# Order of expert weight loads and of the first chunk's statistics, and one filling of the expert slots, in a graph network kernel

## The reference

```python
edge_index = jnp.stack([src, dst])
x = x + L0_gnn(layernorm(x), edge_index, ...)    # two graph convolutions
x = x + L0_ffn(layernorm(x), ...)                # 8 experts, 2 of them for each row
x = x + L1_gnn(layernorm(x), edge_index, ...)    # two graph convolutions
x = x + L1_ffn(layernorm(x), ...)                # shared MLP and 4 gated experts

def _sage_conv(x, src, dst, Wl, bl, Wr):
    agg = jax.ops.segment_sum(x[src], dst, num_segments=N_NODES)
    cnt = segment_sum(ones, dst)
    return (agg / jnp.maximum(cnt, 1.0)[:, None]) @ Wl.T + bl + x @ Wr.T

# L0_ffn: E, H, K = 8, 512, 2
_, idx = jax.lax.top_k(x @ Wg + bg, K)
mask = jax.nn.one_hot(idx, E).sum(axis=-2)
h = jax.nn.gelu(einsum('td,edh->teh', x, W1) + b1, approximate=False)
y = einsum('teh,ehd->ted', h, W2) + b2
out = einsum('ted,te->td', y, mask)              # the two chosen experts, not weighted
```

## Time and profile before

| what | us |
|---|---|
| median of 3 runs | 1549.06 (1548.07 to 1551.01) |
| the profiled execution, in all | 1556.26 |
| its span | 1554.6 |
| TensorE busy, share of the span | 1290.9, 83% |
| VectorE busy | 577.4, 37% |
| ScalarE busy | 404.1, 26% |
| GpSimd busy | 165.4, 11% |

### The profile page before, as it was taken

One profiled execution on the slowest core, in us unless ns is written; L12 is line 12 of the kernel. 1 busy time (PEld: TensorE's weight loads), 2 busy tenths in 40 slices (PEclk: granted clock), 3 DMA queues, 4 the chain that ended last, 5 costly groups with the idle time before them and its releaser, 6 DMA issues. The chain is left out here.

```text
span 1554.6 us, 22266 instructions
## 1 busy us (share of the span) xinstructions
PE 1290.9 (83%) x7949; PEld 950.3 (61%) x7949; DVE 577.4 (37%) x1434; ACT 404.1 (26%) x812; POOL 165.4 (11%) x176
## 2 busy tenths in 40 slices
PE   3675999997999895497868946999978999969998
PEld 3454777774557663376757834655545578746665
DVE  6537777762436546000000005300024352343333
ACT  1343444431111000353233612310011101023332
POOL 3000000000000415142322420000000000000000
PEclk9697999998999987698888987999989999979999
DMA  4333000004543214344343441110044432161000
GB/s 121 117 131 116 15 15 15 15 8 105 151 134 102 96 65 154 100 85 87 79 108 78 68 79 60 69 43 24 24 113 145 142 115 79 62 176 64 17 17 32
DMA packets 134030, 125.25 MB, mean 81 GB/s; under 512 B 22468, under 2 KB 120933, under 8 KB 133955
## 3 DMA queue, kind: packets, MB, share of 16 engines
q1 hardware_dynamic: 99716, 76.35, 16.8%
q0 software_dynamic: 12048, 18.79, 6.1%
q10 hardware_dynamic: 22192, 29.11, 5.3%
HBM read 70.86 MB, written 53.36 MB: 80 GB/s over the span
## 5 line engine op out<-in xcount | busy, mean ns | idle before, releaser
L1012 PE MATMUL b_pa<-adj,b_parts 128*128 (+1 forms) x1100 | 144.6, 286 | 1.9 <-ACT b_sums L934 1.9
L949 ACT ACTIVATE adj<-b_pw 128x450 f32 (+1 forms) x176 | 87.1, 550 | 137.9 <-PE b_pw L1001 137.9
L1012 PEld LDWEIGHTS b_pa<-adj,b_parts 128*128 128x128 f16 x1100 | 105.4, 98 | 26.3 <-ACT adj L949 2.0
L1894 DVE TENSOR_TENSOR e_y<-e_py,l_parts 128x512 f32<-128x512 f32 x28 | 19.4, 691 | 271.5 <-PE e_py L1837 271.5
L1837 PE MATMUL e_py<-l_parts,e_h 128*128 128x256 f32 x448 | 115.4, 416 | 3.3 <-ACT e_h L1879 0.6
L839 DVE TENSOR_TENSOR b_sel<-b_it,b_key 128x1800 f16<-128x1800 f16 x88 | 96.3, 1094 | 49.0 <-PE b_pw L1001 47.7
L1001 PE MATMUL b_pw<-b_sel,b_low 128*128 128x150 f16 x1056 | 86.0, 233 | 30.0 <-DVE b_low L839 17.4
L1837 PEld LDWEIGHTS e_py<-l_parts,e_h 128*128 128x128 f32 x448 | 91.9, 210 | 22.2 <-ACT e_h L1879 8.6
L1827 PE MATMUL e_ph<-e_xt,l_parts 128*128 128x256 f32 x448 | 103.0, 383 | 2.7 <-ACT e_xt L1874 2.7
L1575 PE MATMUL l_sum<-l_parts,adj 128*128 128x256 f16 x750 | 95.4, 286 | 10.5 <-issue 10.3
L1001 PEld LDWEIGHTS b_pw<-b_sel,b_low 128*128 128x128 f16 x1056 | 76.3, 100 | 37.0 <-DVE b_low L839 34.0
(11 more groups left out here) (315 smaller groups left out, 1786.6 us busy)
## 6 DMA issues: line engine op xcount, KB each, us to landing
l_parts<-in_L_ffn_W SPq DMA_DIRECT2D x16, 512.0 KB, 4.7
e_xr<-slots_in SPq DMA_DIRECT2D x28, 257.0 KB, 2.8
sums_and_zt<-n_zt ACTq DMA_DIRECT2D x10, 640.0 KB, 3.1
l_ring<-sums_and_zt SPq DMA_DIRECT2D x25, 256.0 KB, 3.5
l1b_ring<-sums_and_zt SPq DMA_DIRECT2D x25, 256.0 KB, 3.5
n_rows<-in_x SPq DMA_DIRECT2D x5, 640.0 KB, 4.9
parts<-n_part ACTq DMA_DIRECT2D x5, 640.0 KB, 4.3
b_parts<-parts SPq DMA_DIRECT2D x5, 640.0 KB, 7.6
```

Of the source, the lines that this page charges most:

```text
L949: ins = nc.scalar.activation(adj[:, :, ds(group * GW * W + b * BANKW * W, BANKW * W)].rearrange("p k (w j) -> p w k j", j=W), pw[u % SLOT ...
L1012: ins = nc.tensor.matmul(pa[f][:, :], parts[:, k, a, f * P:(f + 1) * P], adj[:, k, ds(r * BW, BW)], start=k == 0 and a == 0, stop=k == TIL ...
```

## The change

There are three changes, and some smaller things that go with them.

1. In `experts`, SyncE issues the next expert's weights after all row loads of the expert, not after its first one.
2. In `Normalise.vector`, the statistics of chunk 0 come ahead of the squared weights. `first_block` keeps its order, with the chain's start written out there.
3. All slots are filled once, with zeros and dump labels, in 12 DMAs of 2304 slots each that ScalarE issues during the first body of the counting, one or two after each group's copies; one more DMA sets the dump rows to zero. GpSimd makes the source, one row of 257 floats in each partition, which the DMAs repeat. ScalarE waits for all of them at the end of the block. `Route.clear`, `tail` and what they need are gone. A filled slot's label is now ROWS + its partition in both halves of a tile, so two slots of a tile share a label. In `experts`, ScalarE makes for each half t the value Relu(label - (ROWS - 1 + t)), and GpSimd adds it to the label instead of copying the label; for labels of real rows it is 0.

Beside these, the tables of the routing are released before `weigh_and_sum`, and the tile `rows` of `second_conv` has MOST instead of CT tiles of rows.

```diff
     def vector(self, dve):
+        self.ch = Chain(dve, self.s["n_chain"])
+        self.vector_norm(dve, 0)
         self.vector_squares(dve)
-        self.vector_norm(dve, 0)
         self.vector_scales(dve)
...
+            nc.gpsimd.iota(dump_i[:, :], pattern=[[1, 1]], base=ROWS, channel_multiplier=1).then_inc(s["dump_ready"], 1)
+            nc.gpsimd.memset(empty[:, 0:D], 0.0).then_inc(s["dump_ready"], 1)
+            pool.wait_ge(s["dump_ready"], 2)
+            nc.gpsimd.tensor_copy(empty[:, D:DW], dump_i[:, :]).then_inc(s["empty_ready"], 1)
...
+            def fill(n):
+                if n == 0:
+                    act.wait_ge(s["empty_ready"], 1)
+                    act.dma_start(g["x1"][ROWS:ROWS + ST, :].rearrange("(r p) d -> p r d", p=P),
+                                  empty[:, 0:D].unsqueeze(1).broadcast_to([P, ST // P, D])).then_inc(s["dump_filled"], 16)
+                rows = E0 * CAP // FILLS
+                to = g["slots_in"][n * rows:(n + 1) * rows, :].rearrange("(b p) d -> p b d", p=P)
+                act.dma_start(to, empty[:, :].unsqueeze(1).broadcast_to([P, rows // P, DW])).then_inc(s["filled"], 16)
...
                 for u in range(UNROLL):
                     take_counts(0, u)
+                    for n in range(FILLS * u // UNROLL, FILLS * (u + 1) // UNROLL):
+                        fill(n)
...
+            act.wait_ge(s["filled"], 16 * FILLS)
+            act.wait_ge(s["dump_filled"], 16)
...
-                table.clear(sp, 0, zero)
...
-                table.clear(act, 1, zero)
...
-    def clear(self, eng, u, zero):
...
-            at = eng.value_load(self.tail[0:1, e:e + 1], min_val=0, max_val=E0 * CAP - ST)
-            eng.dma_start(self.g["slots_in"][ds(at, ST), :].rearrange("(p r) d -> p (r d)", p=P),
-                          zero.rearrange("p r d -> p (r d)")).then_inc(s[f"cleared{u}"], 16)
...
-        nc.vector.tensor_tensor(self.tail[:, :], g["counts"][:, :], self.base_i[:, :], ALU.add).then_inc(s["tail_ready"], 1)
-        nc.vector.memset(zero[:, :, 0:D], 0.0).then_inc(s["zeroed"], 1)
-        dve.wait_ge(s["zeroed"], 1)
-        nc.vector.tensor_copy(zero[:, :, D:DW].rearrange("p r a -> p (r a)"), dump_i[:, :]).then_inc(s["zero_ready"], 1)
...
                 load(at)
-                if 1 <= e < E0 - 1:
-                    u = (e + 1) % 2
-                    sp.wait_ge(s[f"w_free{u}"], (e + 1) // 2)
-                    load_expert(sp, io, weights, e + 1, u, s[f"w_in{u}"])
                 end = sp.value_load(g["tiles"][0:1, 2, ds(e, 1)], min_val=1, max_val=STMAX)
                 with sp.If(tiles > 1):
                     with sp.Fori(at + 1, end) as j:
                         load(j)
                 with sp.Else():
                     sp.nop()
+                if 1 <= e < E0 - 1:
+                    u = (e + 1) % 2
+                    sp.wait_ge(s[f"w_free{u}"], (e + 1) // 2)
+                    load_expert(sp, io, weights, e + 1, u, s[f"w_in{u}"])
...
-                    nc.scalar.activation(ids[:, ds(j * NT, NT)], xr[:, :, D:DW].rearrange("p t a -> p (t a)"), ACT.Copy
-                                         ).then_inc(s["ids_ready"], 1)
+                    nc.scalar.activation(ids[:, 0, ds(j * NT, NT)], xr[:, :, D:DW].rearrange("p t a -> p (t a)"), ACT.Copy)
+                    for t in range(NT):
+                        ins = nc.scalar.activation(ids[:, 1, ds(j * NT + t, 1)], xr[:, t, D:DW], ACT.Relu, bias=above[:, t:t + 1])
+                    ins.then_inc(s["ids_ready"], 1)
...
-                nc.gpsimd.tensor_copy(ids_now[:, :], ids[:, ds(j * NT, NT)]).then_inc(s["ids_now"], 1)
+                nc.gpsimd.tensor_tensor(ids_now[:, :], ids[:, 0, ds(j * NT, NT)], ids[:, 1, ds(j * NT, NT)], ALU.add
+                                        ).then_inc(s["ids_now"], 1)
```

More of the change, by code:

```diff
@@ L1148, in second_conv @@
         late = split(ring[:, :], dict(t=2 * CT), "t d")
-        x0 = pr.sb("rows", [P, CT, DW], F32)
+        x0 = pr.sb("rows", [P, MOST, DW], F32)
         HOME = {0: 0, 1: 0, 2: MOST, 3: 0, 4: 0, 5: MOST, 6: 2 * MOST}
@@ L1521, in _ @@
             act.wait_ge(s["x_out"], 16 * FINISHES)
-            if routing:
-                table.clear(act, 1, zero)
             if not routing:
@@ L1694, in take @@
             return room[:, at:at + n].rearrange(f"p ({' '.join(names)}) -> p {' '.join(names)}", **dict(zip(names, shape)))
-        self.ones, self.down, self.step = take(E0), take(E0), take(STMAX)
+        self.ones, self.step = take(E0), take(STMAX)
         self.cnt, self.past, self.moved = take(6, E0), take(STMAX, E0), take(STMAX)
-        self.base_i, self.down_i = pr.sb("base_i", [P, E0], I32), pr.sb("down_of_i", [P, E0], I32)
         self.step_i, self.cnt_i = pr.sb("step_i", [P, STMAX], I32), pr.sb("cnt_i", [P, 2, E0], I32)
-        self.tail = pr.sb("tail", [P, E0], I32)
@@ L1701, in __init__ @@
-        self.s = {n: pr.sem("r_" + n) for n in ("iotas", "chain", "zeroed", "zero_ready", "tail_ready", "dump_out", "cleared0", "cleared1",
-                                                "tables_ready", "first_w_in0", "first_w_in1")}
+        self.s = {n: pr.sem("r_" + n) for n in ("iotas", "chain", "tables_ready", "first_w_in0", "first_w_in1")}
     def gpsimd(self):
         nc, s = self.nc, self.s
-        nc.gpsimd.iota(self.base_i[:, :], pattern=[[CAP, E0]], base=0, channel_multiplier=0).then_inc(s["iotas"], 1)
@@ L1707, in gpsimd @@
-        nc.gpsimd.iota(self.down_i[:, :], pattern=[[-1, E0]], base=E0, channel_multiplier=0).then_inc(s["iotas"], 1)
         nc.gpsimd.iota(self.step_i[:, :], pattern=[[1, STMAX]], base=0, channel_multiplier=0).then_inc(s["iotas"], 1)
-    def clear(self, eng, u, zero):
-        s = self.s
-        eng.wait_ge(s["zero_ready"], 1)
-        if u:
-            eng.dma_start(self.g["x1"][ROWS:ROWS + ST, :].rearrange("(p r) d -> p r d", p=P), zero[:, :, 0:D]
-                          ).then_inc(s["dump_out"], 16)
-        eng.wait_ge(s["tail_ready"], 1)
-        for e in range(u * E0 // 2, (u + 1) * E0 // 2):
-            at = eng.value_load(self.tail[0:1, e:e + 1], min_val=0, max_val=E0 * CAP - ST)
-            eng.dma_start(self.g["slots_in"][ds(at, ST), :].rearrange("(p r) d -> p (r d)", p=P),
-                          zero.rearrange("p r d -> p (r d)")).then_inc(s[f"cleared{u}"], 16)
-        eng.wait_ge(s[f"cleared{u}"], 16 * E0 // 2)
-        if u:
-            eng.wait_ge(s["dump_out"], 16)
@@ L1726, in vector @@
-    def vector(self, dve, zero, dump_i):
+    def vector(self, dve):
         nc, g, s = self.nc, self.g, self.s
         cnt, cnt_i, past = self.cnt, self.cnt_i, self.past
+        EACH = [P, STMAX, E0]
+        steps = self.step.unsqueeze(2).broadcast_to(EACH)
+        of_experts = lambda ap: ap.unsqueeze(1).broadcast_to(EACH)
         ch = Chain(dve, s["chain"])
-        dve.wait_ge(s["iotas"], 3)
-        nc.vector.tensor_tensor(self.tail[:, :], g["counts"][:, :], self.base_i[:, :], ALU.add).then_inc(s["tail_ready"], 1)
-        nc.vector.memset(zero[:, :, 0:D], 0.0).then_inc(s["zeroed"], 1)
-        dve.wait_ge(s["zeroed"], 1)
-        nc.vector.tensor_copy(zero[:, :, D:DW].rearrange("p r a -> p (r a)"), dump_i[:, :]).then_inc(s["zero_ready"], 1)
+        dve.wait_ge(s["iotas"], 1)
@@ L1735, in vector @@
         ch.mark(nc.vector.memset(self.ones, 1.0))
-        ch.mark(nc.vector.tensor_copy(self.down, self.down_i[:, :]))
         ch.mark(nc.vector.tensor_copy(self.step, self.step_i[:, :]))
@@ L1771, in experts @@
         xr = pr.sb("xr", [P, NT, DW], F32)
-        ids = pr.sb("ids", [P, STMAX * NT], I32)
+        ids = pr.sb("ids", [P, 2, STMAX * NT], I32)
+        above = pr.sb("above", [P, NT], F32)
         ids_now = pr.sb("ids_now", [P, NT], I32)
@@ L1897, in expert @@
                 dve.sem_inc(s[f"w_free{u}"], 1)
+            for t in range(NT):
+                nc.vector.memset(above[:, t:t + 1], -float(ROWS - 1 + t)).then_inc(s["above_ready"], 1)
             dve.sem_inc(s["y_done"], 1)
@@ L2184, in program @@
         build_counts(nc, io, g, adj)
-        for name, shape in (("choice", [P, 2, TILES]), ("counts", [P, E0])):
-            g[name] = held.enter_context(nc.sbuf_tensor(name, shape, F32))
-        g["place"] = held.enter_context(nc.sbuf_tensor("place", [P, 2, TILES], I32))
-        for name, shape in (("tiles", [P, 3, E0]), ("from", [P, STMAX])):
-            g[name] = held.enter_context(nc.sbuf_tensor(name, shape, I32))
-        with nc.sbuf_tensor("l0_parts", [P, TILES, 2, D], F16) as parts:
+        with ExitStack() as tables:
+            for name, shape in (("choice", [P, 2, TILES]), ("counts", [P, E0])):
+                g[name] = tables.enter_context(nc.sbuf_tensor(name, shape, F32))
+            for name, shape in (("place", [P, 2, TILES]), ("tiles", [P, 3, E0]), ("from", [P, STMAX])):
+                g[name] = tables.enter_context(nc.sbuf_tensor(name, shape, I32))
+            parts = tables.enter_context(nc.sbuf_tensor("l0_parts", [P, TILES, 2, D], F16))
```

25 lines of the change are left out of this document (13 added, 12 removed).

## The result

The changed kernel takes 1581.77 us (median of 4, 1576.30 to 1586.63) against 1549.01: ratio 1.0209, 95% interval 1.0173 to 1.0244. It is slower by 32.8 us. I had forecast 1549, no change, and held a loss of that size to be the fourth rival (1578, chance 0.17).

The account below looks back on a forecast made before the run. Experts bound by TensorE's waits for rows, counting by VectorE, then TensorE. Gains 48.6 + 5.0 + 6.1 = 59.7 against 60 lost to the fill cancel: forecast 1549 us, range 1500 to 1582.

Parts of the forecast that it names:

- fourth rival: Counting's fill: unaligned 1028-byte rows stream slower than 345 GB/s, near 247; loss 89 us, time 1578, chance 0.17.
- The bound and its cause: Experts' stage: TensorE loses 50.2 us to waits for rows and half clock, as SyncE issues weights ahead of rows.
- fifth rival: Experts' stage: stalls stay because the weights' small descriptors still hold rows; half the gain gone, 1573, chance 0.12.
- The way the fill costs: Counting: from the second or third fill, issues hold ScalarE for the drain, delaying its ninth evacuation and TensorE; 60 us lost.
- The bytes are hidden: Counting: the fill's 28.4 MB cost nothing themselves, since TensorE's counting lasts until 365.
- Rivals 1 and 2: Counting's fill: short issues, 0.4 to 0.5 us, 1490, chance 0.15; or descriptor making, 3.0 us a fill, 1511, chance 0.08.
- a store of 1024-byte rows drains at about 345 GB/s: Counting's fill: drain rate used to price it, last issue returning at about 209, 60 us lost.
- my own case: Whole kernel: fill draining at 345 GB/s, with either rule for when an issue returns, 1541 to 1558, chance 0.38.
- Experts: Experts' stage: weights behind rows remove all six stalls, less label arithmetic; net gain 48.6 us, bounds 42 and 50.
- Nothing new is late: Experts' stage: with the new load order, rows and weights still arrive in time; two-tile experts have just enough.
- Clears: End of routing: without clears, GpSimd's last scatter is what is late next; gain 5.0 us, bounds 3.5 and 6.5.
- Statistics: Head of second normalisation: statistics ahead of squared weights let TensorE start sooner; gain 6.1 us, bounds 2 and 8.

Follow-up runs that it names:

- experiments 3 and 4: 3: the spread kernel, ratio 0.9660. 4: changed kernel with all 12 fills issued by GpSimd at the head of the counting, 1481.89 us, ratio 0.9676.
- spread kernel: Changed kernel with 18 fills of 1536 slots, two in each of the counting's first nine bodies, instead of 12 of 2304 in the first: 1496.68 us, ratio 0.9660.
- experiment 6: Four variants of the spread kernel, real fills in the last nine bodies, plus a ScalarE burst of 12 stores varying row length and spacing: ratios 0.9964 to 1.0177.
- two-set kernel: Spread kernel with fills in two sets of nine whose labels are already distinct, without Relu or GpSimd's add: 1493.65 us, ratio 0.9650.
- experiments 1 and 7: 1: kernel before with only the experts' weights issued behind all row loads, 1507.8 us, ratio 0.9725. 7: the two-set kernel, 1493.65 us, ratio 0.9650.

## Why the prediction was wrong

**What held.** The bound and its cause: with the weights behind the rows all six inner waits for rows go, and the two-tile experts have margin enough; the fifth rival (chance 0.12) is out. SyncE's row loads behind expert 5's weights come as seven and then two, so expert 6 has 7 tiles and expert 7 has 2, not the other way round; no term of the sum hangs on that. Nor on the rows' landing in the second normalisation: 926.06 + 6.5 is 932.6, not 932.3. The way the fill costs: issues that stall from the second on, ScalarE's ninth copy late by the hold, TensorE two groups behind it, nothing given back. The bytes are hidden, as experiments 3 and 4 show. Rivals 1 and 2 (short issues; a price per descriptor made) are out by the 8.85 us of a fill in the burst and the 0.38 us of one in the spread kernel.

**The step that failed: the term "a store of 1024-byte rows drains at about 345 GB/s", taken for rows of 1028 bytes.** It gave the last issue's return at 209 and a loss of 60; it was 232.5 and 85. With 1024-byte rows the same burst returned at 207.4 (200.57 + 6.84 in that kernel's timeline) and cost 61: the sum was right for a row that the change doesn't write. With the measured 272 GB/s put into it, ten or eleven fills are through at 224 to 233. What makes these rows slower is that 63 in 64 of them start off a multiple of 256 bytes (experiment 6). I had the sign of it in rival 4 (247 GB/s with full engines, "start unaligned and stream slower"), and gave it 0.17 because scatters were part of that row. It was the only row of before with 1028-byte rows and busy engines, so it was the nearer one, and the forecast ought to have been 1578. That the stated range, up to 1582, still holds the 1581.77 is owed to that rival and not to my own case, which ended at 1558.

**The gains were some 5 us smaller than said.** 59.7 forecast; the spread kernel has 53.1 and the two-set kernel 54 to 56. Experts: 48.6 forecast; 46.1 in the changed kernel against the profile of before, 45.1 between the two profiles with the old and the new order (257.5 and 212.4), 42 (39.5 to 45.7) in time. I had 210.6 from first to last turn, and the changed kernel has 213.1. Of these 2.5 us, 1.8 are the interval of 9.57 ahead of expert 6: "Nothing new is late" looked at rows and weights and left out the adds to `x1`, on which VectorE waits. Another 0.6 is the first interval (8.70, not 8.14). The even experts' first intervals are 1.5 us over 7.74 in all, near the 1.2 forecast, but by luck: I had put them down to the labels, and they are there without label arithmetic too (experiments 1 and 7); ScalarE reloads tables there, and in the profile of before these intervals lay under the stalls. What the labels themselves cost is too small for these profiles. Clears: 5.0 forecast, 8.2 measured (5.3 to 11.0) for all that goes with the fill, of which some 3 are where I had put them. Statistics: 6.1 forecast, 5.7 measured (2.9 to 8.7).

60 - 59.7 became 85 - 53, which is the 32 us that the kernel lost.

## What to carry to other kernels

A DMA issue is free only while its queue has room (0.38 us in the spread kernel); past that the issuing engine waits at the drain rate (8.85 us in the burst). Fills that nobody needs soon belong on an engine that nobody waits for, or spread so that each finds the earlier ones drained: the same 28 MB cost 85 us or nothing. Price a transfer by a row of the same length and the same alignment: one float behind a power of two made 63 rows in 64 start off a 256-byte boundary and took a fifth of the rate (346 to 276 GB/s).

The version that beats both: the spread kernel, with or without two sets of labels or Gelu's table first, at 0.965 to 0.966 of before, some 53 us faster than before and 85 faster than the changed kernel; the fill from GpSimd, at 0.968, is the same within the intervals.

## What the runs showed of the hardware

- From ScalarE's queue 2304 rows of 1024 bytes take 6.74 us when every row starts at a multiple of 256 bytes of DRAM and 8.62 when rows start 1028 bytes apart (47 and 60 ns a row on each of 16 engines); 1028 bytes at aligned starts take 6.98. 1152 rows of 2048 bytes take 5.60, at 409 GB/s.
- ScalarE's queue took 0.48 us for a fill of 2304 descriptors with 256 ahead of it, and held the next for 6.17. GpSimd's queue took seven such fills at 1.22 us each, then held GpSimd for 62 us; it moved the unaligned 1028-byte rows at 290 GB/s in 2901 packets of 4.0 KB on the mean, ScalarE's at 260 in 10181 packets of 1.0 KB.
- A DMA that stores from one source row again and again runs as fast as an ordinary store (346 against 345 GB/s).
- In the changed kernel an indirect add of 128 rows to DRAM landed 3.8 us after its issue in the median, and 7.3 at the longest, where an expert's weights were under way beside it.
